# Routed tiles of a mixture-of-experts kernel: one load per tile, a flag table in three pieces, other places for the expert splits, and the experts' down biases added by VectorE

## The reference

```
x = x + tanh(g_xattn) * (attention(ln(x), ln(ctx)) @ Wo + (silu(gate) * h) @ Wff2)
z = layernorm(x)                                   # 2048 tokens
shared = silu(z @ sh_up_w + sh_up_b) @ sh_down_w + sh_down_b
top 2 of 8 experts per token, softmax weights scaled to sum 1 -> comb
y  = sum over the two chosen e of comb[e] * (silu(z @ up_w[e] + up_b[e]) @ down_w[e] + down_b[e])
out = x + tanh(g_ffn) * (y + shared)
```

## Time and profile before

| | |
|---|---|
| median of 3 runs | 556.55 us (554.71 to 557.39) |
| the profiled execution | 554.62 us, span 552.8 us |
| mean granted TensorE clock | 0.976 |
| busy: PE, DVE, ACT, POOL | 501.9, 397.3, 329.7, 285.9 us |
| instructions | 14145 |

### The profile page before, as it was taken

One profiled execution on the slowest core, in us unless ns is written; L12 is line 12 of the kernel. 1 busy time (PEld: TensorE's weight loads), 2 busy tenths in 40 slices (PEclk: granted clock), 3 DMA queues, 4 the chain that ended last, 5 costly groups with the idle time before them and its releaser, 6 DMA issues.

```text
span 552.8 us, 14145 instructions
## 1 busy us (share of the span) xinstructions
PE 501.9 (91%) x4017; PEld 485.4 (88%) x4018; DVE 397.3 (72%) x1179; ACT 329.7 (60%) x1074; POOL 285.9 (52%) x307
## 2 busy tenths in 40 slices
PE   1679999999999999999999999999999949998990
PEld 1669899999999999999999999999987849998990
DVE  6678878788777878877786887877687874554540
ACT  2457656665665656567565666656756716766760
POOL 4347636443532644354264444436666964478773
PEclk9989999999999999999999999999999977999996
DMA  6453400100000000000000000000985554678773
GB/s 186 132 155 115 131 4 28 34 2 11 30 19 0 30 29 0 10 31 19 1 30 29 0 10 30 1 0 31 321 252 170 192 171 77 106 114 128 120 95 40
DMA packets 41607, 39.88 MB, mean 72 GB/s; under 512 B 9939, under 2 KB 39588, under 8 KB 41444
## 3 DMA queue, kind: packets, MB, share of 16 engines
q1 hardware_dynamic: 33276, 27.63, 16.8%
q0 software_dynamic: 7968, 11.84, 11.5%
q10 hardware_dynamic: 330, 0.02, 0.0%
HBM read 20.55 MB, written 18.94 MB: 71 GB/s over the span
## 4 chain that ended last, share of the span: by engine, by line
PE 60%; DVE 17%; DMA 7%; issue 6%; ACT 6%; POOL 1%; DVEq 0%; SPq 0%; POOLq 0%; ACTq 0%
PE bank L1515 12%; PE bank L1516 11%; PE bank L1517 11%; DMA out_x<-norm_probs,th 6%; PE bank L1596 4%; PE bank L1693 4%; PE bank L1608 4%; PE bank L1683 3%; DVE norm_probs L993 3%; PE bank L1599 2%; PE bank L1612 2%; PE bank L1530 2%; PE bank L1698 2%; ACT norm_probs L793 2%; DVE nmax L1130 2%
## 5 line engine op out<-in xcount | busy, mean ns | idle before, releaser
L611 POOL TENSOR_TENSOR norm_probs<-norm_probs,rden 128x512 f32<-128x512 f32 x64 | 66.6, 1040 | 118.4 <-DVE rden L1174 117.7
L1515 PE MATMUL bank<-acts,weights 128*128 128x256 f32 x384 | 110.5, 288 | 3.9 <-DVE weights L1048 3.5
L1516 PE MATMUL bank<-acts,weights 128*128 128x256 f32 x384 | 108.8, 283 | 0.0
L1517 PE MATMUL bank<-acts,weights 128*128 128x256 f32 x384 | 108.5, 283 | 0.0
L793 ACT ACTIVATE norm_probs<-bank,nmax 128x128 f32<-128x128 f32 x256 | 90.6, 368 | 29.2 <-DVE nmax L1130 29.1
L616 POOL TENSOR_TENSOR acts<-uf,acts 128x256 fp32r<-128x256 f32 x64 | 47.6, 744 | 72.0 <-ACT acts L785 72.0
L1515 PEld LDWEIGHTS bank<-acts,weights 128*128 128x128 f32 x384 | 73.2, 191 | 4.8 <-issue 3.6
L720 POOL DMA_INDIRECT out_x<-norm_probs,th x39 | 60.5, 1552 | 30.6 <-DMA out_x<-norm_probs,th 19.8
L1516 PEld LDWEIGHTS bank<-acts,weights 128*128 128x128 f32 x384 | 73.3, 191 | 0.0
L1517 PEld LDWEIGHTS bank<-acts,weights 128*128 128x128 f32 x384 | 73.2, 191 | 0.0
L785 ACT ACTIVATE acts<-uf 128x256 fp32r<-128x256 f32 x64 | 26.8, 418 | 71.5 <-DVE uf L1199 71.4
(11 more groups left out here) (254 smaller groups left out, 1543.2 us busy)
## 6 DMA issues: line engine op xcount, KB each, us to landing
slot_rows<-tf SPq DMA_DIRECT2D x8, 680.0 KB, 6.0
spare<-slot_rows SPq DMA_DIRECT2D x39, 128.0 KB
ct<-in_ctx SPq DMA_DIRECT2D x8, 256.0 KB, 2.8
xs<-in_x SPq DMA_DIRECT2D x8, 256.0 KB, 4.5
out_x<-xs POOLq DMA_DIRECT2D x3, 512.0 KB, 3.7
stage<-in_L_ffn_up_w SPq DMA_DIRECT2D x5, 256.0 KB, 2.7
stage<-in_L_ffn_down_w SPq DMA_DIRECT2D x5, 256.0 KB, 3.2
xs<-in_L_xattn_Wff SPq DMA_DIRECT2D x4, 256.0 KB
```

Source lines behind the costliest of these rows:

```text
L611: pool.tensor_tensor(pr[:, s % 2], pr[:, s % 2], rden[:, s % 2, :].unsqueeze(2).broadcast_to((P, 4, P)), ALU.mult).then_inc(probs_ready, 1)
L1515: pe.matmul(ps, wts[1], mov[0], start=first, stop=False, skip_group_check=True)
L1516: pe.matmul(ps, wts[0], mov[0], start=False, stop=False, skip_group_check=True)
L1517: return pe.matmul(ps, wts[0], mov[1], start=False, stop=last, skip_group_check=True)
```

## The change

- The load of a tile becomes one transfer of all 272 columns. DVE then copies the tile's pair from the loaded rows into `meta`, at an address that depends on the expert, ahead of the lo part of tile t+2. The load of tile t now waits for that lo part (`xg_ready`) instead of the transposes. DVE loads its first `experts_of` at step -2 instead of 0, and the word holds 8 tiles instead of 6.
- PE's bias matmul in the tiles is dropped. DVE adds the down bias, broadcast to all partitions, into a buffer `y_biased` (two of them in SBUF) at the end of its step, and counts `down_biased`. ACT's L936 waits for that and reads the buffer instead of the bank.
- `turn_table` is cut in three pieces, in steps 0, 1 and 2; POOL waits for it ahead of the send of tile 1 instead of tile 0.
- ACT makes `expert_hi(2)` at the end of the last iteration, and `expert_hi(5)` and `(6)` ahead of `hidden_hi(2)`. POOL makes `expert_lo(4)` ahead of the last four routed sends, and each later one a place earlier against the stores.
- In the prologue the split of the 16 expert bias rows is dropped; one row of the shared expert is left. SP broadcasts two bias tables of 8 KB to 128 partitions instead of one.

```diff
-        rows_g = spare[:, 0:4 * D].rearrange("p (s n) -> p s n", s=4)
+        rows_g = spare[:, 0:4 * ROW].rearrange("p (s n) -> p s n", s=4)
+        y_biased = [slow_stage[:, 512 + D * i:512 + D * (i + 1)] for i in range(2)]
...
@@ SP, load_tile
-                packed = sp.value_load(tile_row[0:1, bass.ds(t, 1)], ...)
-                unit = sp.snap(packed >> 4)
-                sp.dma_start(rows_g[:, slot_of, :], by_tile[bass.ds(unit, 1), :, 0:D]...
-                sp.dma_start(meta[:, bass.ds(t, 1), :]..., pairs_by_tile[bass.ds(unit, 1), :, ...]...
+                unit = sp.value_load(tile_row[0:1, bass.ds(t, 1)], ...)
+                sp.dma_start(rows_g[:, slot_of, :], by_tile[bass.ds(unit, 1)].rearrange("a p n -> p (a n)")
...
-                    sp.wait_ge(gT_filled, i * WINDOW + j)
+                    sp.wait_ge(xg_ready, i * WINDOW + j)
@@ POOL
             expert_lo(3)
+            expert_lo(4)
             pool.wait_ge(slots_done, NG + 1)
...
-            expert_lo(4)
             expert_lo(5)
+            expert_lo(6)
             store_tiles(1)
-            expert_lo(6)
+            expert_lo(7)
             store_tiles(2)
-            expert_lo(7)
+            expert_lo(8)
             store_tiles(3)
-            expert_lo(8)
-            pool.wait_ge(turns_done, 1)
...
                 pool.wait_ge(y_copied, t + 1)
+                if t == 1:
+                    pool.wait_ge(turns_done, 1)
@@ ACT
+                    if s == NU + 1 and last:
+                        expert_hi(2)
                     if s >= 2:
                         attended_hi(u - 2, first and s == 2)
...
-            expert_hi(2)
             hidden_hi(0)
...
             second_exp(NG - 1)
-            hidden_hi(2)
-            hidden_hi(3)
             expert_hi(5)
             act.wait_ge(ff2_done, NG * NU)
             expert_hi(6)
+            hidden_hi(2)
+            hidden_hi(3)
...
                 if runs(t - 2):
-                    act.wait_ge(tile_down_filled, t - 1)
+                    act.wait_ge(down_biased, t - 1)
...
-                    act.activation(ys[:, y_at], bank[6 + c % 2][:, 0:D], ACT.Copy, scale=weight)...
+                    act.activation(ys[:, y_at], y_biased[c % 2], ACT.Copy, scale=weight)...
@@ DVE, tile_step
                 if runs(t + 2):
                     dve.wait_ge(xgh_done, t + 3)
+                    e = dve.snap((experts_of >> (SHIFT * (k + 4))) & (NE - 1))
+                    dve.tensor_copy(meta[:, t + 2, :] ..., rows_g[:, (c + 2) % 4, bass.ds(e * 2 + D, 2)])
                     dve.tensor_tensor(xg[1][:, c % 2], ...
...
-                if isinstance(t, int) and t == 0:
-                    turn_table()
+                if loop is None and t in (0, 1, 2):
+                    turn_table(t)
...
+                if runs(t - 2):
+                    e = dve.snap((experts_of >> (SHIFT * k)) & (NE - 1))
+                    dve.wait_ge(tile_down_filled, t - 1)
+                    if not (isinstance(t, int) and t < 4):
+                        dve.wait_ge(y_copied, t - 3)
+                    dve.tensor_tensor(y_biased[c % 2], bank[6 + c % 2][:, 0:D], down_bias[:, bass.ds(e * D, D)],
+                                      ALU.add).then_inc(down_biased, 1)
@@ PE, tile_step
-                        pe.wait_ge(y_copied, t - 3)
-                    add_bias(b, e * D)
+                        pe.wait_ge(down_biased, t - 3)
                     for kt in range(KT):
                         done = matmul3(b, [x[c % 2][:, kt, :] for x in hsT],
-                                       [expert_w(e)(2 + a, kt, 0, D) for a in range(2)], False, kt == KT - 1)
+                                       [expert_w(e)(2 + a, kt, 0, D) for a in range(2)], kt == 0, kt == KT - 1)
```

More of the change, by code:

```diff
@@ L224, in program @@
         experts = weights[:, 2048:]
[L227 to L228 removed]
+        shared_brow = acts[:, 0:D]
+        up_bias, down_bias = [acts[:, D + NE * D * i:D + NE * D * (i + 1)].bitcast(F32) for i in range(2)]
+        y_biased = [slow_stage[:, 512 + D * i:512 + D * (i + 1)] for i in range(2)]
         biased = [u1, uf]
@@ L488, in _ @@
             for a in range(2):
[L489 to L492, removed]
+                sp.dma_start(bias_rows[a], xmT[a][32:33, 0, (NB - 2) * P:NB * P].bitcast(F32)).then_inc(bias_stored, 16)
+            for i, v in enumerate((up_b, down_b)):
+                sp.dma_start(bias_copy[i], v).then_inc(bias_copied, 16)
             load_ctx(2)
@@ L935, in tile_step @@
                         act.wait_ge(y_added[j], i * 16)
-                    act.activation(ys[:, y_at], bank[6 + c % 2][:, 0:D], ACT.Copy, scale=weight).then_inc(y_copied, 1)
+                    act.activation(ys[:, y_at], y_biased[c % 2], ACT.Copy, scale=weight).then_inc(y_copied, 1)
             tile_loop(act, tile_step)
@@ L1086, in _ @@
             dve.tensor_tensor(gw_t[:, 1], gate_cols, gw_t[:, 0].bitcast(F32), ALU.subtract).then_inc(gw_done, 1)
[L1089 to L1093, removed]
+            dve.wait_ge(dbrow_in, 16)
+            place = [t[32:33, 0, (NB - 2) * P:NB * P] for t in xmT]
+            dve.tensor_copy(place[0], dbrow).then_inc(bias_split, 1)
             dve.wait_ge(bias_split, 1)
-            for r in (slice(0, 5 + NE), slice(32, 33 + NE)):
-                done = dve.tensor_tensor(place[1][r, :], all_rows[r, :], place[0][r, :].bitcast(F32), ALU.subtract)
-            done.then_inc(bias_split, 1)
+            dve.tensor_tensor(place[1], dbrow, place[0].bitcast(F32), ALU.subtract).then_inc(bias_split, 1)
             def attended_lo(u):
@@ L1403, in tables @@
                 link(dve.tensor_reduce(tile_sum, tile_cmp, AX.X, ALU.add))
-                dve.scalar_tensor_tensor(tile_row, iota_tile, 16.0, tile_sum, ALU.mult, ALU.add).then_inc(tables_done, 1)
+                dve.tensor_tensor(tile_row, iota_tile, tile_sum, ALU.add).then_inc(tables_done, 1)
             def window_table():
-                first = tile_e[:, 0:WINDOW * NWIN].rearrange("p (w k) -> p w k", k=WINDOW)
-                after = tile_e[:, WINDOW:WINDOW * NWIN].rearrange("p (w k) -> p w k", k=WINDOW)
@@ L1410, in window_table @@
-                dve.tensor_tensor(by_window[:, :, 0:WINDOW], first,
-                                  shares[:, 0:WINDOW].unsqueeze(1).broadcast_to((1, NWIN, WINDOW)), ALU.mult)
-                dve.tensor_tensor(by_window[:, NWIN - 1, WINDOW:], tile_e[:, 0:2], tile_e[:, 0:2], ALU.subtract)
-                link(dve.tensor_tensor(by_window[:, 0:NWIN - 1, WINDOW:], after[:, :, 0:2],
-                                       shares[:, WINDOW:].unsqueeze(1).broadcast_to((1, NWIN - 1, 2)), ALU.mult))
+                for half in range(2):
+                    at = WINDOW * half
+                    done = dve.tensor_tensor(
+                        by_window[:, :, at:at + WINDOW],
+                        tile_e[:, at:at + WINDOW * NWIN].rearrange("p (w k) -> p w k", k=WINDOW),
+                        shares[:, at:at + WINDOW].unsqueeze(1).broadcast_to((1, NWIN, WINDOW)), ALU.mult)
@@ new lines, in turn_table @@
+            def turn_table(part):
+                if part == 0:
+                    dve.wait_ge(ring_ready, NPOS - 3)
+                    link(dve.tensor_scalar(floor_0, ntiles, -float(P), 2.0 * P, ALU.mult, ALU.add))
+                    dve.scalar_tensor_tensor(floor_1, floor_0, -float(P), hist[1][0:1, :], ALU.add, ALU.add)
+                    link(dve.tensor_tensor(floor_0, floor_0, hist[0][0:1, :], ALU.add))
+                    link(dve.tensor_tensor(floor_0, floor_0, floor_1, ALU.max))
+                    link(dve.tensor_tensor(late[:, 1:], early[:, 1:], floor_0[:, 0:NE - 1], ALU.max))
+                    link(dve.tensor_scalar(shared_turn[:, 1:], late[:, 1:], 0.0, 16.0, ALU.is_gt, ALU.mult))
+                elif part == 1:
+                    link(dve.tensor_tensor(by_expert, iota_tile.unsqueeze(2).broadcast_to((1, NTAB, NE - 1)),
+                                           ends[:, 0:NE - 1].unsqueeze(1).broadcast_to((1, NTAB, NE - 1)), ALU.is_equal))
+                    link(dve.tensor_tensor(by_expert, by_expert,
+                                           shared_turn[:, 1:].unsqueeze(1).broadcast_to((1, NTAB, NE - 1)), ALU.mult))
+                else:
+                    link(dve.tensor_reduce(turn_f, by_expert, AX.X, ALU.max))
+                    dve.tensor_copy(turn, turn_f).then_inc(turns_done, 1)
```

108 lines of the change are left out of this document (44 added, 64 removed).

## The result

The changed kernel takes 565.43 us (median of 4 runs, 565.06 to 565.76), the kernel before beside it 555.63 us (4 runs, 554.67 to 557.39): ratio 1.0175, 95% interval 1.0154 to 1.0196. That is slower by 1.75%, 9.8 us where +8.9 was predicted, and at 565.5 almost to the point. The sum behind it was less exact than its result: several terms were off, in both directions, and the base that they were added to was 0.9 us above the later median of the kernel before. That the two times agree to 0.1 us is luck.

The account below looks back on a forecast made before the run. The prediction took PE to bound the kernel now, with 56.7 of 59.7 us busy in the loop. Its terms, +13.6 - 1.5 - 3.6 + 1.0 - 0.6 = +8.9 us on 556.55, gave 565.5 us, range 552 to 577.

Parts of the forecast that it names:

- the ring: Tiles: ACT and DVE wait for each other, each tile costs the whole round, 2.62 us in the loop; 13.6 us more.
- the end: After the tiles: POOL catches up, its last send follows its `ys` by about 1.4 us instead of 2.9; 1.5 less.
- the first tiles: Up to the first `ys`: table in pieces, earlier loads, less the new add; 3.6 us earlier, bounds 1 and 6.
- the splits: Routing chain ahead of the tiles: `expert_lo(4)` now runs beside it; 1.0 us later, bounds 0 and 2.5.
- the prologue: Prologue: two of four small operations and some copies go where DVE sets the pace; 0.6 us less, bounds 0 and 0.8.
- The bounds of the step: Round per tile: all lower bounds give 2.15 us, all upper 2.95; for the tiles 81.3 and 104 us.
- the 1.73: Last four steps up to the last `ys`, with no row tile to split: 1.73 us each, 6.9 together.
- The 4.13 us gap: First tiles: PE's wait up to 456.51 for tile 1's silu, whose bias add stands behind the table; forecast to go.
- its clock: Rival, tiles: PE's clock falls because it is busy only 1.86 of 2.6 us; some 590 us and more, chance 0.03.
- collision: Rival, tiles: DVE's copy of the pair waits for POOL's sends; 17 us, 582 us in all, chance 0.07.
- The short ring: Rival, tiles: address work is done ahead, the round is 2.15 to 2.35 us; 552 to 557.5 us, chance 0.12.
- The other side: Rival, tiles: queues overlap, the round falls under PE's 2.0 us, the removed product is gained whole; 547 us, chance 0.10.

Follow-up runs that it names:

- e17: The changed kernel with the flag table whole in DVE's step 0, as before the change, instead of in three pieces: 564.9 us, 1.0207 of the kernel before.
- e7: The changed kernel with POOL's splits of the experts' weights at their old places: 569.9 us, 1.0290 of the kernel before.
- e3: The changed kernel with DVE copying the pair ahead of its wait for ACT's hi part, all work kept: 553.9 us, 0.9969 of the kernel before.
- e1: The changed kernel without the experts' down bias anywhere, so the output lacks it: 550.1 us, 0.9903 of the kernel before.
- e2: The changed kernel with ACT's `ys` one step later, behind the hi part of tile t+2, all work kept: 554.4 us, 0.9981 of the kernel before.
- e8: The changed kernel with the experts' down biases still products on PE, ACT scaling from the bank, the rest kept: 554.1 us, 0.9966 of the kernel before.
- e12: The changed kernel with the pair copied early and every tile's step written out without the loop: 548.8 us, 0.9866 of the kernel before.

## Why the prediction was right, step by step

The profiled spans, 552.8 and 563.7, are 10.9 us apart. Four marks divide them: POOL's L608 near 400 us (L616 before; 398.84, 400.04), the second group of routed sends (428.56, 431.40), the first `ys` and the last `ys`. Between them the changed kernel takes 1.2 + 1.6 - 4.3 + 12.3 + 0.1 = 10.9 more. The sum forecast 8.9. Measured less forecast, its terms are off by -1.3 (the ring), +1.6 (the end), -0.7 (the first tiles), +0.6 (the splits) and +1.8 (the prologue), +2.0 in all. The medians are only 9.8 apart, and the kernel before, 556.55 when I predicted, is 555.63 with its fourth run: so the two times met.

- **The ring, +13.6: right, 12.3.** Mechanism and size held. ys to hi part was 0.42 for 0.50; hi part to copy 0.77 for 0.67; copy to lo part 0.08 for 0.10; the two DVE steps 0.33 for 0.34; from the add to `ys` 0.65 for 0.67. The turn of the loop, which the sum left out, is 0.15 per four tiles, and makes up for most of the shorter round: 73.3 us in the loop for 73.4. The steps written out are 2.27 for 2.42, the last four 6.5 for 6.9. The bounds of the step don't follow from those of its parts, which give about 2.1 and 3.0, and with them the bounds of the tiles would be wider than 81.3 and 104; the forecast doesn't hang on them.
- **The end, -1.5: wrong, 0.** I had it follow its `ys` by 1.4 us. The last send (554.18) follows the last `ys` (550.75 + 0.51) by 2.9 us, as before. POOL does catch up in the loop (a send starts 2.0 behind the start of its `ys`), but the last four `ys` come 1.6 us apart on average, faster than its 1.85, and from tile 34 on it falls behind again, to 3.4. I had the 1.73 in the sum and did not hold it against the 1.85.
- **The first tiles, -3.6: size about right, cause wrong.** From the second group of sends to the first `ys` the kernel gains 4.3. I ascribed 2.9 to the cutting of the table; e17 gives 0.3 for that. The gain is the splits that no longer run beside the table, and SP's earlier load. The 4.13 us gap did go; the longest wait that PE has there now is 0.85.
- **The splits, +1.0: size about right, instruction wrong.** 1.6 us were lost in the routing chain, to `expert_lo(3)`, not to `expert_lo(4)`. The rows lead on to `expert_hi(2)`, of which I had said that it costs nothing because ACT is idle: it let POOL start earlier, and so beside DVE. I had seen that POOL stretches DVE's small operations, looked only for where that would get worse, and did not look where it would stop: in the table, of which I had a row that was already three times too long (0.47 for 0.17). e7 puts the whole move at 1.1% in favour, where my text has a cost.
- **The prologue, -0.6: not seen.** At 400 us the changed kernel is 1.2 us late. The mark lies between 398.3 and 401.7 in the profiled executions of all kernels here, so that is no finding.
- **Rivals.** PE is at full clock (1.00) and 83% busy by the modelled ends (I said about 70%), so neither PE nor its clock sets the pace. The copy takes 0.17 us in the loop beside the sends (once 0.48), and a send 1.55 on average, as before: no collision, in either direction. The short ring is not what this kernel has; e3 made it by moving one copy, with a step of 2.13.
- **The other side** ("PE stays the bound", 547) was worth less than I gave it: even with the product gone and nothing in its place (e1) the kernel is at 550, since the turn of the loop takes over, and behind it the sends.

## What to carry to other kernels

When work moves from the engine that is full to one that is half idle, draw the waits of both engines through a step before counting busy time: if the new operation waits for the last of one engine and the next step's first waits for it, every operation between costs its full time, and the idle share says nothing. An instruction that such a round doesn't need (an address, a small copy) belongs ahead of the wait. And list what comes second, with its distance: here the sends could not be done in less than 79.7 us of the 83.1 that they took, and what a shorter tile can gain ends there.

## What I had not expected of the hardware

- In the flag table 1x8 operations of DVE took 0.43 to 1.39 us beside POOL's subtractions and 0.15 to 0.17 without; pairs of 128x256 and 128x512 took 1.73 and 2.36 instead of 0.83 and 1.27.
- The turn of the loop costs 0.8 us per four tiles before (steps of 2.77 against 1.97), about 1.2 with the ring open (e2) or the bias on PE in e8, 0.6 in e3 and 0.15 under the long ring, which hides it. Writing the steps out removed it, and the longer code showed no cost of its own: each step of e12 is 1.93, as the steps that e3 had written out already.
- ACT's `ys` takes 0.51 us reading SBUF and 0.47 reading a bank.
